# A graph attention layer on one core: how x and the first two weight tiles arrive, and who makes two low parts

## The reference

```python
q = x @ wq.T + bq;  k = x @ wk.T + bk;  v = x @ wv.T + bv
q2 = (q @ wiq.T + biq)   # k2, v2 alike, split into 16 heads of 64
scores = einsum('hnd,hmd->hnm', q2, k2) / 8 + mask   # mask from the edges' types, -inf where there is no edge
out = einsum('hnm,hmd->hnd', softmax(scores), v2)
result = layernorm(x + out @ wo.T + bo)
```

## Time and profile before

| | |
|---|---|
| runs, median (lowest to highest) | 296.95 us (296.94 to 297.93), 3 runs |
| profiled execution: its time | 296.42 us |
| profiled execution: span, first to last instruction | 294.7 us |
| TensorE matmuls busy | 287.6 us, 98% of the span |
| VectorE, ScalarE, GpSimd busy | 189.0, 157.2, 139.7 us |
| TensorE in the chain that ended last | 96% of the span |
| granted TensorE clock, mean | 0.999 |

### The profile page before, as it was taken

How to read it: one execution, slowest core, us unless ns; L and a number is a source line. 1 busy time by engine, 2 the same in 40 slices (tenths; PEclk the granted TensorE clock), 3 DMA queues, 4 the chain that set the end, 5 groups by cost and what they waited for, 6 DMA issues and landing times.

```text
span 294.7 us, 5253 instructions
## 1 busy us (share of the span) xinstructions
PE 287.6 (98%) x1688; PEld 268.5 (91%) x1688; DVE 189.0 (64%) x474; ACT 157.2 (53%) x299; POOL 139.7 (47%) x124
## 2 busy tenths in 40 slices
PE   7999999999999999999999999999999999999992
PEld 7999999999999998888999999999999998788882
DVE  4879977667666765203257778786878786852184
ACT  4863234423443252421077777777777777673432
POOL 2000644635556551559954454545463636845600
PEclk9999999999999999999999999999999999999999
DMA  7979555453662348925210403031312122410013
GB/s 215 375 229 350 193 178 207 140 166 122 211 218 83 133 143 323 319 74 187 107 65 8 143 11 134 19 125 31 112 42 100 63 80 69 152 67 2 0 71 142
DMA packets 14318, 39.83 MB, mean 135 GB/s; under 512 B 3200, under 2 KB 4832, under 8 KB 14176
## 3 DMA queue, kind: packets, MB, share of 16 engines
q1 hardware_dynamic: 12192, 38.38, 37.8%
q0 software_dynamic: 1680, 0.62, 1.0%
q10 hardware_dynamic: 432, 0.66, 0.8%
HBM read 37.44 MB, written 2.21 MB: 135 GB/s over the span
## 4 chain that ended last, share of the span: by engine, by line
PE 96%; DMA 1%; DVE 1%; ACT 1%; issue 0%
PE bank L880 23%; PE bank L871 20%; PE bank L873 19%; PE bank L872 19%; PE bank L974 6%; PE bank L957 5%; PE bank L945 5%; DMA w_raw<-weights 1%; ACT res L565 0%; DVE w_lo L598 0%; ACT w_hi L404 0%; DVE x_lo L605 0%; DVE stats L845 0%; DVE res L844 0%; DVE mean_var L847 0%
## 5 line engine op out<-in xcount | busy, mean ns | idle before, releaser
L337 POOL DMA_INDIRECT mask_cells<-cell_value,cell x48 | 52.1, 1085 | 76.5 <-DMA mask_cells<-cell_value,cell 32.8
L308 POOL TENSOR_TENSOR w_lo<-w_raw,w_hi 128x1024 fp32r<-128x1024 f32 x20 | 47.6, 2404 | 43.9 <-DVE probs L768 40.7
L871 PE MATMUL bank<-x_hi,w_hi 128*128 128x384 f32 x192 | 64.3, 335 | 0.5 <-DVE x_lo L605 0.5
L872 PE MATMUL bank<-x_lo,w_hi 128*128 128x384 f32 x192 | 64.1, 334 | 0.0
L873 PE MATMUL bank<-x_hi,w_lo 128*128 128x384 f32 x192 | 64.1, 334 | 0.0
L394 ACT ACTIVATE w_hi<-w_raw 128x1024 fp32r<-128x1024 f32 x50 | 52.3, 1052 | 19.1 <-PE bank L880 18.1
L871 PE MATMUL bank<-h_hi,w_hi 128*128 128x384 f32 x128 | 47.2, 369 | 0.0
L592 DVE TENSOR_TENSOR w_lo<-w_raw,w_hi 128x1024 fp32r<-128x1024 f32 x30 | 36.6, 1224 | 12.5 <-ACT w_hi L394 10.1
L440 ACT ACTIVATE h_hi<-bank,bcol 128x384 f32 (+1 forms) x24 | 14.0, 582 | 56.9 <-PE bank L873 56.9
L873 PE MATMUL bank<-h_hi,w_lo 128*128 128x384 f32 x128 | 43.1, 337 | 0.0
L872 PE MATMUL bank<-h_lo,w_hi 128*128 128x384 f32 x128 | 42.9, 335 | 0.0
(11 more groups left out here) (94 smaller groups left out, 496.0 us busy)
## 6 DMA issues: line engine op xcount, KB each, us to landing
w_raw<-weights SPq DMA_DIRECT2D x54, 512.0 KB, 3.3
probs<-key_rows SPq DMA_DIRECT2D x6, 512.0 KB, 4.1
res<-x_rows SPq DMA_DIRECT2D x1, 1536.0 KB, 6.7
out<-res SPq DMA_DIRECT2D x6, 256.0 KB, 2.0
v<-x_t SPq DMA_DIRECT2D x6, 192.0 KB, 5.8
w_raw<-weights SPq DMA_DIRECT2D x3, 256.0 KB, 6.0
mask_cells<-cell_value,cell POOLq DMA_INDIRECT x48, 3.1
mask_cells<-mask SPq DMA_DIRECT2D x1, 576.0 KB, 4.5
```

What stands on the lines that cost most here:

```text
L308: nc.gpsimd.tensor_tensor(lo, w_raw[:, s, cols], hi.bitcast(F32), ALU.subtract)\
L337: nc.gpsimd.indirect_dma_start(out=mask_cells, out_offset=bass.IndirectOffsetOnAxis(ap=cell[:, c:c + 1], axis=0), in_=cell_value[:, c:c + ...
L871: pe.matmul(out_ps, w_hi[:, s, cols], moving_hi, start=(k == 0), stop=False)
L872: pe.matmul(out_ps, w_hi[:, s, cols], moving_lo, start=False, stop=False)
```

## The change

x's block k and the columns of tiles 0 and 1 that meet it come as one block of 320 KB (`start[k]`: 384 + 2 x 128 columns), eight of them, alternately on the two queues; block 0 is cut in two pieces, the weights' 128 KB on SP and x's 192 KB on ScalarE's queue. The raw blocks lie in a buffer `shared` that `v2` and `probs` are now parts of, so the first key rows wait for the blocks' low parts. Each block is split by itself, weights first. TensorE takes a block's six matmuls in the order high times high, low weight times high x, high weight times low x, each for both tiles, and waits ahead of each pair only for what it reads. Warm-up matmuls are 9 instead of 16. Tile 2 comes, is split and is waited for in halves, behind block 7 and ahead of the edge tables. VectorE, not GpSimd, makes the low parts of pair tiles 32 and 33 (`POOL_TILE` is 34).

```diff
+POOL_TILE = PAIR_TILE + LEAD
-WARM_UP = 16
+WARM_UP = 9
+START = N + FIRST_TILES * P
...
+        shared = sb("shared", [P, NT * F + 2 * NT * N], F32)
+        v2_flat = shared[:, 0:NT * F]
+        probs_flat = shared[:, NT * F:NT * F + 2 * NT * N]
+        def start_raw(k):
+            return shared[:, START * k:START * (k + 1)]
...
 # SP's queue
-            half_tile(0, 0)
-            x_block(1)
-            x_block(2)
-            half_tile(0, 1)
-            half_tile(1, 1)
-            for k in range(4, KT):
-                x_block(k)
+            sp.dma_start(start_raw(0)[:, N:START], start[0, :, N:START]).then_inc(first_w_loaded, 16)
+            start_block(1)
+            start_block(3)
+            for k in range(5, KT):
+                start_block(k)
+            for h in range(2):
+                third_tile(h)
             sp.dma_start(er[:, :, :], edge_rows).then_inc(edges_loaded, 16)
-            first_tile(2)
...
-                if t - RING >= PAIR_TILE:
-                    sp.wait_ge(w_lo_pool, t - RING + 1 - PAIR_TILE)
+                if t - RING >= POOL_TILE:
+                    sp.wait_ge(w_lo_pool, t - RING + 1 - POOL_TILE)
...
             sp.wait_ge(scratch_stored, 16)
+            sp.wait_ge(w_lo_dve, FIRST_TILES)
+            sp.wait_ge(x_lo_done, KT)
             load_rows(0, 0)
...
 # GpSimd
-            for t in range(PAIR_TILE, PAIR_TILE + LEAD):
-                low_part(t, t % RING)
...
 # ScalarE
-            act.dma_start(x_raw(0), x_t[:, 0, :]).then_inc(x_loaded[0], 16)
-            act.dma_start(w_raw[:, 1, HALVES[0]], weights[1, :, HALVES[0]]).then_inc(first_half_loaded[1], 16)
-            act.dma_start(x_raw(3), x_t[:, 3, :]).then_inc(x_loaded[3], 16)
+            act.dma_start(x_raw(0), start[0, :, 0:N]).then_inc(start_loaded[0], 16)
+            for k in (2, 4):
+                act.dma_start(start_raw(k), start[k, :, :]).then_inc(start_loaded[k], 16)
...
+            def start_high(k):
+                act.wait_ge(start_loaded[k] if k else first_w_loaded, 16)
+                nc.scalar.activation(first_part(w_hi, k), first_raw(k), ACT.Copy)\
+                    .then_inc(*((first_hi, 1) if k < KT - 1 else (w_hi_done, FIRST_TILES)))
+                act.wait_ge(start_loaded[k], 16)
+                nc.scalar.activation(x_hi[:, k, :], x_raw(k), ACT.Copy).then_inc(x_hi_done, 1)
...
+            for k in range(KT):
+                start_high(k)
+            for h in range(2):
+                third_high(h)
...
 # VectorE
+            def start_low(k):
+                dve.wait_ge(*((first_hi, k + 1) if k < KT - 1 else (w_hi_done, FIRST_TILES)))
+                nc.vector.tensor_tensor(first_part(w_lo, k), first_raw(k), first_part(w_hi, k).bitcast(F32),
+                                        ALU.subtract)\
+                    .then_inc(*((first_lo, 1) if k < KT - 1 else (w_lo_dve, FIRST_TILES)))
                 dve.wait_ge(x_hi_done, k + 1)
                 nc.vector.tensor_tensor(x_lo[:, k, :], x_raw(k), x_hi[:, k, :].bitcast(F32),
                                         ALU.subtract).then_inc(x_lo_done, 1)
...
-            for t in range(FIRST_TILES):
-                low_part(t + LEAD, t + LEAD)
-                evacuate(t, t)
+            evacuate(0, 0)
+            low_part(FIRST_TILES + 1, FIRST_TILES + 1)
+            evacuate(1, 1)
             low_part(FIRST_TILES + LEAD, 0)
...
-            for t in range(IV_TILE, PAIR_TILE - LEAD):
+            for t in range(IV_TILE, PAIR_TILE):
                 lows(t)
...
 # TensorE, for k in range(KT)
+                pe.wait_ge(*((first_hi, k + 1) if k < KT - 1 else (w_hi_done, FIRST_TILES)))
+                pe.wait_ge(x_hi_done, k + 1)
+                first_products(w_hi, x_hi)
+                pe.wait_ge(*((first_lo, k + 1) if k < KT - 1 else (w_lo_dve, FIRST_TILES)))
+                first_products(w_lo, x_hi)
                 pe.wait_ge(x_lo_done, k + 1)
+                first_products(w_hi, x_lo)
```

More of the change, by code:

```diff
@@ L60, with gnn_layer @@
 SCALE = 1.0 / 8.0
-def gnn_layer(nc, x_t, x_rows, weights, bias_cols, bias_rows, edge_weights, edge_cols, edge_rows,
+def gnn_layer(nc, start, x_rows, weights, bias_cols, bias_rows, edge_weights, edge_cols, edge_rows,
               key_rows, mask_cells, out):
@@ L166, in gnn_layer @@
         raw_loaded = [sem(f"raw_loaded{s}") for s in range(RING)]
-        x_loaded = [sem(f"x_loaded{s}") for s in range(KT)]
+        start_loaded = [sem(f"start_loaded{k}") for k in range(KT)]
         small_loaded = sem("small_loaded")
@@ L179, in gnn_layer @@
         w_hi_done, w_lo_dve, w_lo_pool = sem("w_hi_done"), sem("w_lo_dve"), sem("w_lo_pool")
-        first_half_loaded = [sem(f"first_half_loaded{t}") for t in range(FIRST_TILES)]
-        first_half_hi, first_half_lo = sem("first_half_hi"), sem("first_half_lo")
+        first_w_loaded = sem("first_w_loaded")
+        first_hi, first_lo = sem("first_hi"), sem("first_lo")
+        third_half_loaded, third_half_hi, third_half_lo = (
+            sem(n) for n in ("third_half_loaded", "third_half_hi", "third_half_lo"))
         tile_done = sem("tile_done")
@@ L606, in x_low, with third_low @@
                                         ALU.subtract).then_inc(x_lo_done, 1)
-            first_low(0, 0)
-            x_low(0)
-            first_low(1, 0)
-            for k in range(1, 4):
-                x_low(k)
-            first_low(0, 1)
-            first_low(1, 1)
-            for k in range(4, KT):
-                x_low(k)
+            def third_low(h):
+                dve.wait_ge((third_half_hi, w_hi_done)[h], (1, FIRST_TILES + 1)[h])
+                nc.vector.tensor_tensor(w_lo[:, FIRST_TILES, HALVES[h]], w_raw[:, FIRST_TILES, HALVES[h]],
+                                        w_hi[:, FIRST_TILES, HALVES[h]].bitcast(F32), ALU.subtract)\
+                    .then_inc((third_half_lo, w_lo_dve)[h], 1)
+            for k in range(KT):
+                start_low(k)
+            for h in range(2):
+                third_low(h)
             dve.wait_ge(edges_loaded, 32)
@@ L861, in tile_ready @@
             def tile_ready(t, pair_tile=False):
-                if pair_tile:
-                    pe.wait_ge(w_lo_pool, t + 1 - PAIR_TILE)
+                if pair_tile and not (isinstance(t, int) and t < POOL_TILE):
+                    pe.wait_ge(w_lo_pool, t + 1 - POOL_TILE)
                 else:
@@ L891, in _, with first_products @@
             for k in range(KT):
[L892 to L900 removed]
+                cols = slice(k * P, (k + 1) * P)
+                def first_products(w, x):
+                    for t in range(FIRST_TILES):
+                        ins = pe.matmul(layer_acc[t][:, 0:N], w[:, t, cols], x[:, k, :],
+                                        start=(k == 0 and w is w_hi and x is x_hi), stop=(k == KT - 1 and x is x_lo))
+                        if k == KT - 1 and x is x_lo:
+                            ins.then_inc(tile_done, 1)
+                pe.wait_ge(*((first_hi, k + 1) if k < KT - 1 else (w_hi_done, FIRST_TILES)))
[3 more added lines that the diff above has]
+                first_products(w_lo, x_hi)
+                pe.wait_ge(x_lo_done, k + 1)
+                first_products(w_hi, x_lo)
             def group(g, slots=range(RING)):
@@ L904, in group @@
                     t = RING * g + s
-                    tile_ready(t)
+                    if isinstance(g, int) and t == FIRST_TILES:
+                        pe.wait_ge(third_half_lo, 1)
+                    else:
+                        tile_ready(t)
                     if not isinstance(g, int):
@@ L910, in group @@
                     for k in range(KT):
+                        if isinstance(g, int) and t == FIRST_TILES and k == KT // 2:
+                            tile_ready(t)
                         ins = by_outputs(layer_acc[s][:, 0:N], s, k, x_hi[:, k, :], x_lo[:, k, :])
@@ L1115 @@
     arrays = {
-        "x_t": x.T.reshape(KT, P, N).transpose(1, 0, 2),
+        "start": np.concatenate([x.T.reshape(KT, P, N), *(weights[t].reshape(P, KT, P).transpose(1, 0, 2)
+                                                          for t in range(FIRST_TILES))], axis=2),
         "x_rows": x.reshape(NT, P, F).transpose(1, 0, 2),
```

65 lines of the change are left out of this document (21 added, 44 removed).

## The result

| | before | after |
|---|---|---|
| median (lowest to highest) | 297.44 us (296.45 to 298.14), 6 runs | 294.84 us (294.53 to 295.16), 6 runs |
| ratio, 95% interval | | 0.9917 (0.9896 to 0.9938) |
| profiled execution: time, span | 296.42, 294.7 us | 295.16, 293.4 us |
| granted TensorE clock, mean | 0.999 | 0.994 |

The changed kernel is 0.8% faster. The forecast, 295.7 us and "within half a per cent", was wrong: 294.84 lies just under the range's lower end of 295.0. In later sessions the kernel before had medians of 296.63 to 296.75, and the changed one beside it 295.15 and 294.88, ratios 0.993 and 0.9932: 1.6 and 1.8 us, not the 2.6 of the table. The two profiled executions differ by 1.26 us, the forecast's 1.25; but the one of before is faster than all six of its runs and the one of after is the slowest of its six, so this agreement is partly luck.

A forecast was written before the change was run, and what follows sets the result against it. TensorE was taken to bound everything but the head; tile 2 starting at 14.25 instead of 15.53 us gains 1.3, taken as 1.25. 296.42 - 1.25 = 295.2, with the median 0.5 above: 295.7 us, range 295.0 to 297.4.

The forecast's parts named there:

- The cap of 1.5 us: Tile 6: slack 0.38 us, plus 0.8, plus 0.3 from an earlier softplus start, limits the gain to about 1.5 us.
- The sum for the profiled execution: Whole kernel: span 294.7 less the 1.25 us gain gives 293.45; time 296.42 less 1.25 gives 295.2 us.
- Read off the same curves: Head loads: landings taken from before's curves, x of block 0 at 5.2 us, block 1 at 6.0, block 2 at 6.8.
- Rival (c): Head loads: all lands 0.9 us sooner, gain 2.2 us, cut by the cap to 1.5, giving 295.4 us; chance 0.13.
- They cost nothing by themselves: Warm-up: nine for sixteen cost 0, end at 4.8 us, with slow steps up to about 4.1 us.
- The runs' median, 296.95, is 0.5 above that execution; I predict for the median: Last step: from the profiled execution's 295.2 us to a predicted median of 295.7 us.
- Term 0: Pair tiles 32 and 33: low parts on VectorE instead of GpSimd are in time in both orders, worth 0.
- rival (e): Pair tiles 32 and 33 matter; excluded by TensorE being busy 32.80 of 32.80 us up to 140.
- for nobody: Behind the pair tiles: GpSimd's additions start about 1 us sooner, with no one waiting for them.
- (a): First stage: blocks 1 and 2 arrive too late at 250 GB/s; gain 0.4, 296.5 us; chance 0.12.
- (b): Tiles 3 to 6: VectorE's chain does not move; cap falls to 0.7 (296.25 us) or 0.38 (296.6); chance 0.10.
- (d): First stage: a 0.95 us pause or nine warm-ups leave TensorE at 1.2 GHz; 297.8 or 299.9 us; chance 0.08.

The follow-up runs named there:

- a_pool2: The changed kernel with the low parts of tiles 32 and 33 back on GpSimd, second session: 295.01 us, ratio 0.9942 to before.
- a_split: The changed kernel with blocks 1 to 7 each loaded in two transfers, 128 KB of weights and 192 KB of x: 295.67 us, ratio 0.9956 to before.
- b_xcontig: The kernel before with x's eight blocks each contiguous in DRAM: 296.8 us, ratio 0.9989 to before.
- a_strided: The changed kernel with the start blocks laid out partition first, a block's rows 20 KB apart in DRAM: 294.9 us, ratio 0.9921 to before.
- a_third: The changed kernel, unchanged, run again as the measure for others on its chip: 294.88 us, ratio 0.9932 to before.
- b_again: The kernel before, unchanged, against itself: 296.72 us, ratio 1.0005.
- b_warm9: The kernel before with 9 warm-up matmuls instead of 16, nothing else: 298.33 us, ratio 1.0062 to before.
- b_late: The kernel before with two more subtractions on GpSimd ahead of tile 32's low part: 297.36 us, ratio 1.003 to before.
- a_rows: The changed kernel with blocks from 1 on still one 320 KB transfer each, in rows of 1.25 KB instead of 2.5 KB: 295.15 us, ratio 0.9943 to before.

## Why the prediction was wrong

*What bounds, and where a gain counts: right.* Span less tile 2's start, all that lies behind the head, is 279.2 us in before and 279.2 in five profiles of unchanged or nearly unchanged after kernels (293.4 - 14.18, 293.2 - 14.00 and the like). Everything gained in the head arrives at the end, and tiles 3 and 6 wait for nothing. The cap of 1.5 us was too low: in a_pool2 tile 2 starts at 13.73 us, 1.80 earlier than in before, and TensorE still doesn't wait at tile 6.

*The sum for the profiled execution: right, by two errors that cancel.* Forecast 293.45, measured 293.4. Block 0 was mis-sized: landed 3.9 instead of 5.2, high parts done at 4.64 instead of 5.72. One step that failed is "Read off the same curves": it took before's landings over, though the transfers had changed. For block 1 the number of transfers matters, as a_split shows: 286 GB/s and a landing at 6.4 us, where after has 5.6. For block 0 it doesn't (3.9 in a_split too). What differs there is the first pair of transfers, 320 KB in after and 448 in before, and how x lies in DRAM; which of them it is stays open: b_xcontig hints at x's layout, a_strided, with rows 20 KB apart and block 0 at 3.9, speaks against it. Rival (c) had the sign. Against it stands the step "They cost nothing by themselves", which let the clock rise at 4.1 us in the changed kernel as well. It rose at 6.7; nine warm-ups ended at 5.35, not 4.8, and the first five distances between products sum to 1.73 us (4.99 to 6.72) where 5 x 0.173 is 0.87. In a_third it rose at about 5.4, yet tile 2 starts at 14.00, only 0.18 earlier, for there block 1 is what is waited for.

*"They cost nothing", further.* What the step costed at zero is a term with both signs. In before, sixteen warm-ups hold the products back when the clock rises late (first product at 7.4, b_again), nine lose 1.6 us, for the products run at 1.2 GHz until 10.5 (b_warm9); in after, nine instead of sixteen give 1.1 us. The Trainium skill, "TensorE: Matmul & The Clock Gate", "What's actually happening", says that the number of matmuls at the lower level changes from run to run of one kernel. The prediction quoted the page for another rule and read a fixed moment out of one profile; the runs agree with the skill: the kernel before has 13 starts of warm-up products 0.21 us or more apart in its first profile and 25 in b_again's.

*From the execution to the median: the step that put the forecast out of its range.* "The runs' median, 296.95, is 0.5 above that execution; I predict for the median" added 0.5 to 295.2. In after the median lies 0.3 under the profiled execution (294.84, 295.16), so the term measured -0.3 instead of +0.5. It was no constant: it is what executions of before differ among each other, by the rise under a long warm-up (296.2 to 297.1) and by the late third (297.4 and over). Both shrink with the change, to a spread of 0.6 us in six runs of after. Without it the sum says 295.2, which is 0.36 us over the measured median.

*The pair tiles: wrong.* Term 0, rival (e) "excluded by TensorE's 32.80 of 32.80 us". That row belongs to one execution, with the mask at 132.45. GpSimd's low part would be in time until the mask's load is about 4 us later. In both profiles of before over 297.4 us it is (136.90 and 136.67), in both under 297 it isn't; the late ones lose 1.0 to 1.2 us, through tile 32 a little and through the additions on `res` mostly. That this is what the whole third has in common is inferred from its times and from b_late. I had followed the low parts to TensorE, and dismissed the additions behind them ("for nobody"), though VectorE's first scores wait for them. In the first session three of six executions of before were late, which is most of why that session shows the largest gain.

*Rivals.* (a) fell: blocks 1 to 3 come in time in most profiles, and where block 1 is late (a_third, a_pool2, a_rows) it costs 0.3 to 0.5 us, in a_third a distance of 0.50 between products instead of 0.17. (b) fell: VectorE's chain moved by 1.45 us. (d) is real in before with nine. In after its pause is gone, because the data comes before the warm-up ends, but its other half came true in small: nine warm-ups had not raised the clock, and the first products lost the 0.86 us above.

*Left open.* What sets the moment of the rise; what delays GpSimd's scatter by 4 us in some executions; and what in the changed kernel keeps it from being late (at most one such execution in 15 with the low parts on GpSimd). What lets block 0 land 1.3 us earlier. Whether it's the count of transfers or their size that lowers the early rate, since each run changed both.

## What to carry to other kernels

A warm-up has to be sized with the moment at which the data arrives: too long holds the products back, too short ahead of late data gives a pause, with the products behind it at 1.2 GHz, and both depend on the execution. One profile shows one execution: where the median stands above it, look at what can be late in the others, and follow every wait behind the work on the late engine, the shared buffers too. In this head, which waits for loads, a few full-width transfers beat many, and each transfer more that ScalarE issued delayed its first instruction by about half a microsecond.

## What the runs showed of the hardware

- The moment at which TensorE's products come closer together (1.2 to 2.4 GHz) varied from 4.1 to 6.8 us in four executions of the unchanged kernel before, all with warm-up products back to back from 1.13 us on, and from 4.0 to 7.2 in 18 profiles; the granted clock was shown as 1.00 over the first 12 us of every one.
- Rows of 1.25 KB or 2.5 KB, and blocks contiguous or 20 KB apart, made no difference to the rate from 4 to 6 us (384 against 383, 406 against 388 and 403 GB/s), though the shorter rows moved 7% less from 2 to 10 us; two 160 KB transfers over 64 partitions each gave 222.
- The start of GpSimd's mask load, behind 48 indirect transfers, lay between 129.3 and 136.9 us in 20 profiles; the three over 134.5 are all of kernels that start from before.
